# Attention cut into single-block steps, with the steps behind it carried on between the expert units

## The chip, the cores and the metric

The kernel is one program on one core of one Trainium2 chip. The metric is the device time of one execution in microseconds (us), median of three. The engines are named as in the profile: PE (TensorE, matrix products and transposes), PEld (its weight loads), DVE (VectorE), ACT (ScalarE), POOL (GpSimd), SP (SyncE, which issues DMAs here). Each engine runs its own instructions strictly in their order and waits for the others through semaphores.

## The reference, cut to what matters

Sixteen batches of 512 rows of 128 numbers, all fp32, go through two residual branches.

```python
h = layernorm(x) * (1 + ca) + sa
x = x + ga * attention(h)      # rows routed to 2 of 8 experts; q, k, v; chunked linear attention per expert,
                               # at most 256 rows of an expert; two parts weighted and summed; norm per head; o_w
h = layernorm(x) * (1 + cb) + sb
x = x + gb * ffn(h)

# ffn(h):
h = h @ lin0_w + lin0_b
h = silu(h @ swi1_w1 + b1) * (h @ swi1_w2 + b2)
scores = softmax(h @ gate_w.T);  topv, topi = top_k(scores, 4);  combine = topv / sum(topv), scattered over 8
g = silu(einsum('td,edh->eth', h, exp_w1)) * einsum('td,edh->eth', h, exp_w3)
routed = einsum('te,etd->td', combine, einsum('eth,ehd->etd', g, exp_w2))
h = routed + silu(h @ sh_w1) * (h @ sh_w3) @ sh_w2      # shared part, 2 x 128 hidden
h = h @ lin1_w + lin1_b
h = silu(h @ swi2_w1 + b1) * (h @ swi2_w2 + b2)
```

## The kernel before

A batch is four tiles of 128 rows. The program is a row of blocks of code (`nc.Block()`); all engines leave one before any enters the next.

1. **Preparation** (lines 241 to 636). Loads, layer norm, q products and logits in 17 steps of one batch each (`steps`, from `step` on each engine), then two rounds of routing on DVE (`route`), which give each row its place. POOL scatters the rows of the first four batches to DRAM, sorted by expert.
2. **Attention** (lines 741 to 1292). The sorted rows make 160 blocks of 128 rows. A loop runs over *pairs* of blocks (`for g in ITERATIONS`). PE turns the rows (`turn`, L966), forms k and v (`keys_values`, L978), turns k (`turn_k`, L985), forms the scores (`scores`, L995, both blocks of a pair at once, into the four banks of `wide`), the state k'v (`states`, L1016), adds the carried state (`carried`, L1027) and the scores times v (`attend`, L1035), and turns the result (L1046). ACT copies from PSUM. DVE masks scores (`mask_scores`, L1142) and q (L1162), multiplies k (L1136) and sums states (L1154); POOL masks the summed state by heads (`sum_masked`, L756), which PE's `carried` needs.
   Once the blocks of a batch are stored, the batch has *later steps*: POOL gathers its rows (L765) and adds halves (L778), ACT weights them, DVE normalises, PE turns, multiplies by `o_w`, `lin0`, the two `swi1` matrices and the router's matrix (L1051, L1058, L1102), DVE adds the residual (L1223) and finishes the hidden rows (L1237). A table `J1` gives each batch a slot; slot = block number, a batch starts its PE steps every `PERIOD` = 10 slots, the first at slot 58, the last at 208, and `at(step, slot)` says which batch has that step there. The blocks end at slot 159, so the loop goes on to slot 226 with later steps alone.
3. **Router** (lines 1316 to 1382). The choice of four experts for the rest of the rows on DVE, exponent and turned weights, the split of all expert weights into a high and a low part (ACT L1335, POOL L1328), the weights to DRAM.
4. **Experts** (lines 1426 to 1570). 160 units, ten a batch (eight experts, two shared halves): PE forms gate and up (`up`, L1471, three matmuls each), ACT applies Silu (L1532), POOL multiplies by the row weights that a DMA has spread over the partitions (L1437), DVE multiplies gate and up (`ep`, L1568), ACT and DVE split the product into high and low (L1537, L1561), PE adds the unit's share three units later (`down`, L1481). The last products of the batch before (`tail`, L1488 to L1498) stand in units 3, 4, 5 and 7.

## Time and profile before

| | us |
|---|---|
| runs of before | 1444.19, 1449.04, 1450.40; median 1449.04 |
| profiled execution, its own time | 1450.58 |
| span of its instructions | 1448.8 |
| PE busy | 1127.1 (78%) |
| DVE busy | 875.1 (60%) |
| ACT busy | 683.7 (47%) |
| POOL busy | 586.2 (40%) |

The span is the time from the first to the last instruction of the profiled execution; 1.8 us of its own time lie around it. Busy shares are averages over four stages of different kinds. The time of a stage is read from the start of its first instruction to that of the next stage, and inside a stage from the distance between two starts of the same line. Mean granted clock of PE: 0.88 of full speed (full is 2.4 GHz, the other level 1.2 GHz).

### The profile page before, as it was taken

What the parts mean: (1) busy time and instruction counts of PE and PEld (TensorE: products, weight loads), DVE (VectorE), ACT (ScalarE), POOL (GpSimd) and SP (SyncE); (2) the same over time, 40 slices, a digit from 0 to 9 for tenths busy, and PEclk for the clock granted to TensorE, in tenths of its full rate; (3) what the DMA queues carried; (4) which work ended last, traced back from release to release, by engine and by line L of the source; (5) the groups of instructions that cost most, each with busy time, mean ns of one, the idle gap of its engine ahead of it and who ended that gap; (6) DMA issues with size and microseconds to landing.
All of it is one profiled execution on the core that took longest, in us unless ns stands there. A gap on an engine that the chain in (4) does not pass through costs nothing. (4 is left out here: it accounts for less than half of the span.)

```text
span 1448.8 us, 27085 instructions
## 1 busy us (share of the span) xinstructions
PE 1127.1 (78%) x9330; PEld 802.7 (55%) x9330; DVE 875.1 (60%) x1823; ACT 683.7 (47%) x1653; POOL 586.2 (40%) x626
## 2 busy tenths in 40 slices
PE   2891118889877888888898885663699999999997
PEld 2671006666655565555666652321477777777774
DVE  5447275666456666665777767325366666666664
ACT  1460004555445565555666653332355555555553
POOL 1003403442555445554333335503245454545541
PEclk8895559999898999999999995555699999999997
DMA  9921112332332222222222111100432332424220
GB/s 310 390 113 47 69 48 77 103 90 78 97 89 83 72 79 87 84 84 66 71 58 67 56 35 29 27 3 0 123 107 83 96 101 78 118 66 131 66 73 14
DMA packets 83536, 125.71 MB, mean 87 GB/s; under 512 B 9041, under 2 KB 65873, under 8 KB 79313
## 3 DMA queue, kind: packets, MB, share of 16 engines
q1 hardware_dynamic: 73168, 98.86, 22.6%
q0 software_dynamic: 10240, 25.18, 5.4%
q8 instruction: 76, 1.25, 0.4%
q14 instruction: 52, 0.42, 0.1%
HBM read 71.32 MB, written 52.69 MB: 86 GB/s over the span
## 5 line engine op out<-in xcount | busy, mean ns | idle before, releaser
L1142 DVE SCALAR_TENSOR_TENSOR att<-reach,endrel,wide 128x1024 f32<-128x1024 f32 x160 | 204.4, 1277 | 197.0 <-PE wide L995 146.1
L1437 POOL TENSOR_TENSOR eg<-eg,hq 128x512 f32<-128x512 f32 x128 | 172.7, 1355 | 211.6 <-ACT eg L1532 183.4
L1561 DVE TENSOR_TENSOR epp<-ep,epp 128x512 fp32r<-128x512 f32 x160 | 148.9, 930 | 131.4 <-ACT epp L1537 129.9
L199 POOL DMA_INDIRECT routed_rows<-hq,idxs x128 | 132.5, 1035 | 189.3 <-DVEq L611 117.3
L756 POOL TENSOR_TENSOR sm<-su,headm 128x128 f32<-128x128 f32 x160 | 76.2, 476 | 289.4 <-DVE su L1154 287.7
L978 PE MATMUL bank<-kvw,turned 128*128 x320 | 148.9, 547 | 32.8 <-DVE kf L1136 25.3
L1481 PE MATMUL bank<-epp,w2p 128*128 128x512 f32 x480 | 156.4, 434 | 2.9 <-DVE epp L1561 2.9
L1537 ACT ACTIVATE epp<-ep 128x512 fp32r<-128x512 f32 x160 | 100.8, 630 | 104.9 <-DVE ep L1568 104.9
L765 POOL DMA_INDIRECT gst<-attended_rows,idxs x128 | 133.5, 1043 | 33.5 <-issue 32.8
L850 ACT ACTIVATE k1s<-bank 128x128 f32<-128x128 f32 x160 | 44.4, 278 | 181.7 <-PE bank L978 173.4
L995 PE MATMUL wide<-turned,kx 32*128 32x128 f32 x2560 | 108.9, 291 | 5.9 <-ACT kx L864 3.6
L1481 PEld LDWEIGHTS bank<-epp,w2p 128*128 128x128 f32 x480 | 89.5, 189 | 40.1 <-issue 21.3
L995 PEld LDWEIGHTS wide<-turned,kx 32*128 32x128 f32 x2560 | 90.2, 189 | 26.0 <-ACT kx L864 16.7
L1471 PE MATMUL bank<-hp,w1p 128*128 128x512 f32 x321 | 93.3, 400 | 9.5 <-DVE ep L1568 5.6
L864 ACT ACTIVATE kx<-bank,parity 128x256 f32<-128x256 f32 x160 | 66.9, 469 | 64.5 <-PE bank L985 62.2
L1035 PE MATMUL bank<-att,vx 128*32 128x128 f32 x2560 | 91.3, 286 | 0.0
L1471 PE MATMUL wide<-hp,w3p 128*128 128x512 f32 x318 | 90.0, 391 | 0.0
L978 PEld LDWEIGHTS bank<-kvw,turned 128*128 128x128 f32 x320 | 48.7, 191 | 59.9 <-issue 52.3
L1532 ACT ACTIVATE eg<-bank 128x512 f32<-128x512 f32 x107 | 62.8, 587 | 31.0 <-PE wide L1471 15.9
L1035 PEld LDWEIGHTS bank<-att,vx 128*32 128x32 f32 x2560 | 68.4, 114 | 12.5 <-issue 6.1
L1471 PEld LDWEIGHTS bank<-hp,w1p 128*128 128x128 f32 x321 | 61.6, 193 | 23.8 <-DVE ep L1568 6.0
L1568 DVE TENSOR_TENSOR ep<-wide,eg 128x512 f32<-128x512 f32 x106 | 72.1, 681 | 0.0
(269 smaller groups left out, 2166.2 us busy)
## 6 DMA issues: line engine op xcount, KB each, us to landing
hq<-weight_rows SPq DMA_DIRECT2D x16, 2048.0 KB, 9.7
routed_rows<-zero SPq DMA_DIRECT2D x4, 5120.0 KB, 24.5
rows<-routed_rows SPq DMA_DIRECT2D x80, 256.0 KB
attended_rows<-ob SPq DMA_DIRECT2D x80, 128.0 KB
out<-fin SPq DMA_DIRECT2D x16, 256.0 KB, 2.5
routed_rows<-hq,idxs POOLq DMA_INDIRECT x128
gst<-attended_rows,idxs POOLq DMA_INDIRECT x128
kw_raw<-in_k_w SPq DMA_DIRECT2D x1, 512.0 KB, 5.3
```

What stands on the lines that cost most here:

```text
L199: pool.indirect_dma_start(hs[s], bass.IndirectOffsetOnAxis(idxs[:, t, k:k + 1], 0), hq[:, t, :], None, bounds_check=BLOCKS[s] * P - 1, oob ...
L756: pool.tensor_tensor(sm[:, n % 4, :], su[:, n % 4, :], headm[:, :], ALU.mult).then_inc(s_sm, 1)
L765: pool.indirect_dma_start(gst[:, u, k, :], None, orow[s], bass.IndirectOffsetOnAxis(idxs[:, b * NT + k // TOPA, k % TOPA:k % TOPA + 1], 0) ...
L978: pe.matmul(bank[1][:, 0:KV], turned[:, n // 2 % 2, 0, n % 2, :], kvw[:, bass.ds(w, KV)], start=True, stop=True).then_inc(s_kv, 1)
L995: mm = pe.matmul(wide[:, p, (2 * a + par) * P:(2 * a + par + 1) * P], kx[r, par, a * P:(a + 1) * P], turned[r, g % 2, 1, a, :], start=True ...
L1035: mm = pe.matmul(bank[2][32 * p:32 * p + 32, n % 2 * P:(n % 2 + 1) * P], vx[:, n % 4, p, par * DK:(par + 2) * DK], att[:, n % 2, p, par * ...
L1142: dve.scalar_tensor_tensor(out=att[:, n % 2, :, :], in0=reach[:, :, :].rearrange("p a c -> p (a c)").unsqueeze(1) .to_broadcast([P, 4, 2 * ...
L1437: pool.tensor_tensor(g, g, rows_of(b % 2, n, n + 1), ALU.mult).then_inc(s_eu, 1)
L1471: mm = pe.matmul(ps[:, :], w[:, wk, n, :], hp[:, b % 2, hk, :], start=(wk + hk == 0), stop=(hk == 1))
L1481: mm = pe.matmul(bank[0][:, :], w2p[:, wk, n, :], epp[:, k % RING, hk, :], start=(n + wk + hk == 0), stop=(n == NU - 1 and hk == 1))
L1537: act.activation(epp[:, (k - 1) % RING, 0, :], ep[:, (k - 1) % RING, :], ACT.Copy).then_inc(s_eh, 1)
L1561: dve.tensor_tensor(epp[:, (k - 1) % RING, 1, :], ep[:, (k - 1) % RING, :], epp[:, (k - 1) % RING, 0, :], ALU.subtract).then_inc(s_el, 1)
```

## The change

- **Attention by blocks.** The loop runs over single blocks (`ITERATIONS = range(-6, NBK)`). Scores are formed and masked one block at a time, in one half of the four banks, one block ahead of `attend`; k and v are formed five blocks ahead of it (three at most before). `rows` and `turned` have three buffers, `kx` two, `vx` six. The head mask goes from the summed state (POOL) to the state before the sum, for two blocks at once, on DVE (`mask_states`). `kf`, `km`, `qm`, `sm` lie in tiles of `hq`, so DVE waits for the first scatters before it clears buffers. The table begins later: first PE steps at slot 86, then every 10 slots.
- **Later steps run on among expert units.** The loop ends at slot 159. `post_pool`, `post_act`, `post_pe`, `post_freed` and `post_dve` are shared functions, and expert unit k calls them with slot 160 + k. The last batch has its router product at slot 252, unit 92. On DVE the steps are cut smaller and spread over more slots, and the adding of halves moves from POOL to DVE.
- **Router by four.** Once four batches have their logits, 33 small DVE operations over the next slots choose and weight them, ACT takes the exponent in between (it needs another table and Silu's again afterwards: four pairs of table loads, three of them among the expert units), PE turns four batches at once. Block 3 is gone.
- **Weights split early.** `w1s`, `w3s`, `w2s` are loaded into the last tiles of `hq`, and ACT (before step 8 of preparation) and POOL split them there; ACT waits for POOL before step 12.
- **Experts.** Gate products have two banks instead of three, since bank 3 belongs to the later steps, so `up(k)` also waits for the Silu of unit k - 2. A step's product or transposes end the unit on PE. POOL makes the hidden rows' parts of batches 0 and 1 at the start of this block.

```diff
+                for n, (w, parts) in enumerate(((w1s, w1p), (w3s, w3p), (w2s, w2p))):
+                    pool.wait_ge(s_wh, n + 1)
+                    pool.tensor_tensor(parts[:, 1, :, :], w[:, :, :], parts[:, 0, :, :],
+                                       ALU.subtract).then_inc(s_wl, 1)
...
-                steps(act, step)
+                def split_weights():
+                    act.wait_ge(s_w1, 16 * NW1)
+                    for w, parts in ((w1s, w1p), (w3s, w3p), (w2s, w2p)):
+                        act.activation(parts[:, 0, :, :], w[:, :, :], ACT.Copy).then_inc(s_wh, 1)
+
+                steps(act, step, split_weights, lambda: act.wait_ge(s_wl, 3))
...
-        PERIOD, GATHER = 10, 16
+        PERIOD, GATHER, CHAIN, ROUTE = 10, 19, 10, 33
+        J1 = [C0[1] + 46 + PERIOD * b for b in range(NB)]
...
-                    pool.tensor_tensor(sm[:, n % 4, :], su[:, n % 4, :], headm[:, :], ALU.mult).then_inc(s_sm, 1)
...
+                def mask_states(g):
+                    dve.wait_ge(s_st, g + 1)
+                    if g:
+                        dve.wait_ge(s_sm, 2 * g)
+                    dve.tensor_tensor(sh[:, :, :], bank[3][:, 0:2 * P].rearrange("p (a c) -> p a c", c=P),
+                                      headm[:, :].unsqueeze(1).to_broadcast([P, 2, P]), ALU.mult).then_inc(s_sh, 1)
...
+                for n in ITERATIONS:
+                    h, odd = divmod(n, 2)
+                    if is_block(n + 1):
+                        scores(n + 1)
+                    if is_block(n):
+                        attend(n)
+                    if not odd and here(h + 1):
+                        states(h + 1, n)
+                    if is_block(n + 5):
+                        keys_values(n + 5)
+                    if not odd and here(h + 3):
+                        turn(h + 3)
+                    if odd and here(h):
+                        turn_outputs(h)
+                    if odd and here(h + 2):
+                        turn_k(h + 2)
+                    if not odd and here(h + 1):
+                        pe.wait_ge(s_sh, h + 2)
+                    post_pe(pe, n)
+                    if is_block(n + 1):
+                        carried(n + 1)
...
-        gate_bank = (bank[1], bank[2], bank[5])
-        up_bank = (bank[3], bank[4], bank[6])
+        gate_bank = (bank[1], bank[2])
+        up_bank = (bank[4], bank[5], bank[6])
...
+                    if k >= 2:
+                        pe.wait_ge(s_es, k - 1)
...
                     if BEHIND <= k < UNITS + BEHIND:
                         down(k - BEHIND)
+                    post_pe(pe, NBK + k)
```

PE in the attention, one pair of blocks without later steps, in the order before (`wide` holds the scores, `kvw` the k and v matrices, `ident` marks a transpose):

```order
L995 MATMUL wide<-turned,kx 128x128 x16
L978 ISA
L978 MATMUL bank<-kvw,turned 128x384
L966 MATMUL bank<-ident,rows 128x128 x4
L1016 MATMUL bank<-vx,km 128x128 x2
L1046 MATMUL bank<-ident,oTs 128x128 x2
L978 ISA
L978 MATMUL bank<-kvw,turned 128x384
L1027 MATMUL bank<-qm,sm 128x128 x2
L985 MATMUL bank<-ident,kf 128x128 x2
L1035 MATMUL bank<-att,vx 32x128 x16
```

And the same pair in the changed kernel, two passes of the loop (`hq` now holds kf, km, qm and sm):

```order
L1235 MATMUL wide<-turned,kx 128x128 x8
L1270 MATMUL bank<-att,vx 32x128 x8
L1253 MATMUL bank<-vx,hq 128x128 x2
L1210 ISA
L1210 MATMUL bank<-kvw,turned 128x384
L1199 MATMUL bank<-ident,rows 128x128 x4
L1262 MATMUL bank<-hq 128x128
L1235 MATMUL wide<-turned,kx 128x128 x8
L1270 MATMUL bank<-att,vx 32x128 x8
L1210 ISA
L1210 MATMUL bank<-kvw,turned 128x384
L1224 MATMUL bank<-ident,oTs 128x128 x2
```

The sixteen score products became two groups of eight, each followed at once by the `attend` of the block before, and `turn_k` (L1217, right behind the last row shown) no longer stands two rows behind the k product that it needs.

PE in the experts, two units of before with nothing of a batch's tail:

```order
L1471 MATMUL bank<-hp,w1p 128x512 x3
L1471 MATMUL bank<-hp,w3p 128x512 x3
L1481 MATMUL bank<-epp,w2p 128x512 x3
L1471 MATMUL bank<-hp,w1p 128x512 x3
L1471 MATMUL wide<-hp,w3p 128x512 x3
```

And four units of the changed kernel (L797 turns, L804 multiplies; both are later steps of another batch):

```order
L1466 MATMUL bank<-epp,w2p 128x512 x3
L797 MATMUL bank<-ident,gst 128x128 x4
L1456 MATMUL bank<-hp,w1p 128x512 x3
L1456 MATMUL wide<-hp,w3p 128x512 x3
L1483 MATMUL wide<-ident,t 128x128 x4
L1466 MATMUL bank<-epp,w2p 128x512 x3
L804 MATMUL bank<-jt,oT 128x512
L1456 MATMUL bank<-hp,w1p 128x512 x3
L1456 MATMUL wide<-hp,w3p 128x512 x3
L1466 MATMUL bank<-epp,w2p 128x512 x3
L797 MATMUL bank<-ident,jm 128x128 x4
```

Eight of ten units end with a piece of a later step.

DVE in the experts, two units of before:

```order
L1561 TENSOR_TENSOR epp<-ep,epp 128x512
L1568 TENSOR_TENSOR ep<-bank,eg 128x512
L1546 SCALAR_TENSOR_TENSOR t<-wide,bias,tg 128x512
L1561 TENSOR_TENSOR epp<-ep,epp 128x512
L1568 TENSOR_TENSOR ep<-wide,eg 128x512
```

And two of the changed kernel, in a batch that also has router pieces (`choice`, `top`; `kvw` now holds eg and ep):

```order
L1549 TENSOR_TENSOR epp<-kvw,epp 128x512
L1556 TENSOR_TENSOR kvw<-wide,kvw 128x512
L958 TENSOR_REDUCE var<-gst 128x32
L962 TENSOR_SCALAR var<-var 128x32
L968 BN_STATS bst<-x_all 128x6 x4
L928 TENSOR_TENSOR choice<-choice,top 128x128
L932 TENSOR_TENSOR choice<-choice 128x128
L934 SCALAR_TENSOR_TENSOR choice<-choice 128x128
L1549 TENSOR_TENSOR epp<-kvw,epp 128x512
L1556 TENSOR_TENSOR kvw<-wide,kvw 128x512
```

The later steps stand between the product of one unit and the split of the next operand.

## Rows read from the trace of the kernel before

**Rows 1.** Windows by stage: us, busy by engine with counts, clock, DMA share, GB/s.

```profile
108.00:209.00 101.00, 13.22 (x132) 9.62 (x132) 61.17 (x150) 2.59 (x5) 32.03 (x32) 0.52 0.12 42
355.00:865.00 510.00, 429.63 (x5307) 307.50 (x5311) 331.66 (x751) 288.35 (x842) 237.55 (x291) 0.97 0.25 74
865.00:993.00 128.00, 84.56 (x209) 37.86 (x198) 52.95 (x181) 45.48 (x101) 39.41 (x37) 0.53 0.07 18
993.00:1026.00 33.00, 3.77 (x17) 2.32 (x17) 23.61 (x34) 7.85 (x9) 12.61 (x7) 0.50 0.03 8
1061.00:1410.00 349.00, 334.90 (x1408) 258.06 (x1407) 233.85 (x310) 189.20 (x337) 183.61 (x141) 1.00 0.31 90
```

**Rows 2.** Timeline, first state sum of block 0 and of block 40: start, duration.

```profile
224.58 0.35 DVE L1154 SCALAR_TENSOR_TENSOR su<-su,carry,bank 128x128 f32<-128x128 f32 x1 [0.88 <-PE bank L1016]
359.84 0.35 DVE L1154 SCALAR_TENSOR_TENSOR su<-su,carry,bank 128x128 f32<-128x128 f32 x1
```

**Rows 3.** Timeline, residual added for batches 0, 9, 11 and 15.

```profile
448.49 0.68 DVE L1223 TENSOR_TENSOR x_all<-bank,x_all 128x512 f32<-128x512 f32 x1
831.20 0.68 DVE L1223 TENSOR_TENSOR x_all<-bank,x_all 128x512 f32<-128x512 f32 x1
889.63 0.69 DVE L1223 TENSOR_TENSOR x_all<-bank,x_all 128x512 f32<-128x512 f32 x1
968.84 0.69 DVE L1223 TENSOR_TENSOR x_all<-bank,x_all 128x512 f32<-128x512 f32 x1 [8.18 <-PE bank L1051]
```

**Rows 4.** Timeline, one pair of blocks without later steps.

```profile
337.31 1.17 PE L995 MATMUL wide<-turned,kx 32*128 32x128 f32 x32
338.55 1.28 DVE L1142 SCALAR_TENSOR_TENSOR att<-reach,endrel,wide 128x1024 f32<-128x1024 f32 x1 [2.04 <-PE wide L995]
340.25 0.79 DVE L1154 SCALAR_TENSOR_TENSOR su<-su,carry,bank 128x128 f32<-128x128 f32 x2
341.11 0.52 PEld L1027 LDWEIGHTS bank<-qm,sm 128*128 128x128 f32 x4 [0.43 <-DVE su L1154]
342.14 0.28 DVE L1136 TENSOR_TENSOR kf<-bank,k1s 128x128 f32<-128x128 f32 x1
342.34 0.60 DVE L1162 SCALAR_TENSOR_TENSOR qm<-column,erel,turned 128x128 f32<-128x128 f32 x2
342.48 0.14 PEld L985 LDWEIGHTS bank<-ident,kf 128*128 128x128 f32 x1 [0.79 <-DVE kf L1136]
343.75 1.17 PE L995 MATMUL wide<-turned,kx 32*128 32x128 f32 x32
```

**Rows 5.** Timeline, starts of expert units around a product, four transposes, and neither.

```profile
1164.45 0.85 PE L1471 MATMUL bank<-hp,w1p 128*128 128x512 f32 x3
1167.39 0.85 PE L1471 MATMUL bank<-hp,w1p 128*128 128x512 f32 x3
1172.40 0.84 PE L1471 MATMUL bank<-hp,w1p 128*128 128x512 f32 x3
1174.89 0.86 PE L1471 MATMUL bank<-hp,w1p 128*128 128x512 f32 x3
1176.95 0.84 PE L1471 MATMUL wide<-hp,w1p 128*128 128x512 f32 x3
```

**Rows 6.** Page, costliest groups: busy us, mean ns, idle before and its releaser.

```profile
L1437 POOL TENSOR_TENSOR eg<-eg,hq 128x512 f32<-128x512 f32 x128 | 172.7, 1355 | 211.6 <-ACT eg L1532 183.4
L1561 DVE TENSOR_TENSOR epp<-ep,epp 128x512 fp32r<-128x512 f32 x160 | 148.9, 930 | 131.4 <-ACT epp L1537 129.9
```

**Rows 7.** Timeline of the router block: weights split, a DVE operation beside it.

```profile
994.88 1.25 ACT L1335 ACTIVATE w3p<-w3s 128x1280 fp32r<-128x1280 f32 x1
995.05 2.89 POOL L1328 TENSOR_TENSOR w1p<-w1s,w1p 128x1280 fp32r<-128x1280 f32 x1 [43.55 <-ACT w1p L1335]
995.28 2.88 DVE L228 TENSOR_TENSOR fw<-fw,fa 128x192 f32<-128x192 f32 x1
997.31 1.28 ACT L1337 ACT_TABLE_LOAD   x1
```

More of the change, by code:

```diff
@@ new lines, in adaln_block @@
+        gst = kept("gst", [P, 2, NT * TOPA, D])
+        NV = NT * H + NT
+        var = kept("var", [P, NV])
+        inv = kept("inv", [P, NV])
+        tmp = kept("tmp", [P, NV])
+        offset = kept("offset", [P, NT])
+        jt = kept("jt", [P, S])
+        jh = kept("jh", [P, S])
+        jm = kept("jm", [P, S])
+        js = kept("js", [P, S])
+        bst = kept("bst", [P, NT, 6])
+        mv = kept("mv", [P, NT, 2])
+        RT = 4 * NT
+        left, one, equal, picked, ex = (kept(f"choice{i}", [P, RT, E]) for i in range(5))
@@ L739, in at, with group, halves_of, post_pool @@
             return b if rest == 0 and 0 <= b < batches else None
-        def here(g):
-            return 0 <= g < PAIRS
-        ITERATIONS = range(-2, LAST // 2 + 1)
-        with nc.Block() as block:
-            @block.gpsimd
-            def _(pool):
-                def sum_masked(n):
-                    pool.wait_ge(s_su, n + 1)
-                    if n >= 3:
-                        pool.wait_ge(s_o, (n - 3) // 2 + 1)
-                    pool.tensor_tensor(sm[:, n % 4, :], su[:, n % 4, :], headm[:, :], ALU.mult).then_inc(s_sm, 1)
-                def gather(b, k):
+        def group(step, slot):
+            b = at(step + 16, slot)
+            return b // 4 if b is not None and b % 4 == 3 else None
+        def halves_of(b):
+            return gst[:, b % 2, :, :].rearrange("p (i s) d -> p i s d", s=TOPA)
+        def post_pool(pool, slot):
+            for k in range(NT * TOPA):
+                b = at(k - GATHER, slot)
+                if b is not None:
                     u, s = b % 2, sum(b >= x for x in B0[1:])
@@ new lines, in adaln_block, with here, is_block, _ @@
+        s_a = sem("scores_masked")
+        s_st = sem("states_ready")
+        s_sh = sem("states_masked")
+        s_sm = sem("states_summed")
+        s_o = sem("attended")
+        s_oc = sem("attended_copied")
+        s_ot = sem("attended_turned")
+        s_oe = sem("attended_rows_ready")
+        def here(g):
+            return 0 <= g < PAIRS
+        def is_block(n):
+            return 0 <= n < NBK
+        ITERATIONS = range(-6, NBK)
+        with nc.Block() as block:
+            @block.gpsimd
+            def _(pool):
+                sent = [NT * TOPA * B0[1]]
+                def scatters(n):
@@ new lines, in turn_k, with turn_outputs, scores @@
+                    mm.then_inc(s_kt, 1)
+                def turn_outputs(g):
+                    pe.wait_ge(s_oc, g + 1)
+                    pe.wait_ge(s_te, min(g + 4, PAIRS))
+                    for a in range(2):
+                        mm = pe.transpose(bank[0][:, (2 + a) * P:(3 + a) * P], oTs[:, a * P:(a + 1) * P], ident[:, :])
+                    mm.then_inc(s_ot, 1)
+                def scores(n):
+                    pe.wait_ge(s_kx, n // 2 + 1)
+                    if n:
+                        pe.wait_ge(s_a, n)
+                    a = n % 2
+                    for par in range(2):
+                        for p in range(4):
+                            r = slice(32 * p, 32 * p + 32)
+                            mm = pe.matmul(wide[:, p, par * P:(par + 1) * P], kx[r, n // 2 % 2, par, a * P:(a + 1) * P],
+                                           turned[r, n // 2 % 3, 1, a, :], start=True, stop=True)
@@ L1018, in states @@
+                    for slot in (n - 2, n - 1):
+                        if group(12, slot) is not None:
+                            pe.wait_ge(s_wc, group(12, slot) + 1)
+                    for m in (2 * g, 2 * g + 1):
+                        pe.wait_ge(s_km, m + 1)
+                        pe.wait_ge(s_ve, m + 1)
+                        mm = pe.matmul(bank[3][:, m % 2 * P:(m % 2 + 1) * P], km[:, m % 4, :], vx[:, m % 6, :, 0:DK],
                                        start=True, stop=True)
@@ new lines, in attend @@
+                def attend(n):
+                    pe.wait_ge(s_a, n + 1)
+                    v = vx[:, n % 6, :, :].rearrange("q h c -> q (h c)")
+                    for par in range(2):
+                        for p in range(4):
+                            mm = pe.matmul(bank[2][32 * p:32 * p + 32, n % 2 * P:(n % 2 + 1) * P],
+                                           v[:, (4 * p + par) * DK:(4 * p + par + 2) * DK],
+                                           att[:, n % 2, p, par * P:(par + 1) * P], start=False, stop=True,
+                                           skip_group_check=True)
+                    mm.then_inc(s_o, 1)
@@ L1429, in _ @@
             def _(pool):
+                for b in range(2):
+                    hidden_parts(pool, b, b)
                 for k in range(UNITS):
@@ L1556, in _ @@
                     b, n = divmod(k, NU)
+                    post_freed(dve, NBK + k)
                     if b:
```

994 lines of the change are left out of this document (445 added, 549 removed).

## Prediction

> **What bounds the kernel now.** I read the windows by stage first [rows 1]. From 355 to 865 us (attention with later steps) PE is busy 84% of the time at a granted clock of 0.97, DVE 65%; in the experts (1061 to 1410) PE is busy 96% at 1.00, DVE 67%. Between them lie 161 us in which nothing is full: 865 to 993, the later steps of the last six batches or so, PE busy 66% at clock 0.53, and 993 to 1026, the router, PE 11%. From 108 to 209 DVE's routing sets the pace (61.17 us busy) and POOL's scatters.
>
> Then the distances of repeated lines. Blocks without later steps: 40 blocks in 359.84 - 224.58 = 135.3 us, 33.8 per ten [rows 2]. With them: nine batches, ninety blocks, in 831.20 - 448.49 = 382.7, 42.5 per ten; later steps alone: (968.84 - 889.63) / 4 = 19.8 per batch [rows 3]. Later steps therefore cost 8.7 us a batch beside blocks and 19.8 alone. In a pair without them (6.44 us from scores to scores) PE's loads wait 0.43 for the state sum, since POOL masks it, and 0.79 for kf; DVE waits 2.04 for the scores [rows 4]. So the pair is a loop of waits, not a full engine.
>
> **The change, part by part.** All of it is against the profiled execution: span 1448.8, own time 1450.6, which is 1.5 above the median of the runs shown; I treat them as equal.
>
> *Work of a pair, first.* PE: 6.44 less the two waits is 5.2 us. DVE: two masks of 1.28, 0.79, two of 0.28 and 0.60 make 4.5 [rows 4]; the new head mask (two blocks, 256 columns, one operand in PSUM) lies between kf's 0.28 (128 columns) and the residual's 0.68 (512) [rows 3, 4], I take 0.42, so 4.9. *Later steps on PE:* a unit with a product lasts 1167.39 - 1164.45 = 2.94, one with four transposes 1174.89 - 1172.40 = 2.49, a plain one 1176.95 - 1174.89 = 2.06 [rows 5]: 0.88 a product, 0.43 a turn. Four products, three turns and the router's eight short matmuls (estimate 0.8) make 5.6 a batch at full clock. *Later steps on DVE:* 52.95 busy in the tail for 6.5 batches, 8.1 a batch with the choices [rows 1]; plus the adding of halves (0.7, as the residual's 0.68), plus about 2 because the choices come in pieces of four batches: 9 to 11.
>
> *Preparation.* ACT's three copies cost 1.25 each, 3.8 us in a loop whose steps follow closely. POOL's three subtractions last 2.9 each, and beside the first a small DVE operation lasted 2.88, as long as POOL's own [rows 7]. In the changed kernel the normalising operations of DVE stand beside them. So between +4 (copies alone) and +12 (copies and all of POOL's 8.7): I take +6.
> The Trainium skill (SBUF — State Buffer, Who interferes with whom) says that a DVE operation with two SBUF inputs is blocked for the whole of a GpSimd instruction that reads SBUF. The row with 2.88 agrees. It speaks against putting these subtractions there.
>
> *Filling the loop.* First state sum 15.6 us after the block began (209 to 224.58) [rows 1, 2]. The new loop has two more single passes before block 0 and clears buffers only after the scatters: 0 to +5, I take +3.
>
> *Attention.* All the waits just named get a block or more of distance: scores are masked while PE does `attend` of the block before, the sum needs no POOL, kf is made a pass ahead. What remains is the larger engine. Later steps reach DVE at slot 77. Until then, 77 blocks at the larger of 2.6 (PE) and 2.45 (DVE) plus some coupling: I take 2.8, 216 us. From there 83 blocks: PE 26 + 5.6 = 31.6, DVE 24.7 + 9 to 11 = 34 to 36 per ten, so DVE becomes the bound there, at 3.5 a block, 291 us. Together 507 against 865 - 224.58 = 640: **-133**. The bounds: PE's work alone is 160 x 2.6 + 7 x 5.6 = 455 (-185); at the old pace with fewer later steps in it, 77 x 3.38 + 83 x 4.25 = 613 (-27).
>
> *The tail and the router.* 128 + 33 = **-161** [rows 1]. The weights' split and the first hidden rows that lay in the router block are the terms above and below.
>
> *Experts.* Slots 160 and later hold 72 of the 128 PE steps (batch 6 has three left, batch 7 five, eight batches all): nine batches' worth. PE is full here, so each costs at least 5.6 (+51). A batch there is 100 matmul records (90, three products of two, four turns), and 1408 of them in 349 us make 24.8 us a batch; DVE's 233.85 make 16.6 of it [rows 1]. Plus 9 to 11 is 26 to 28, plus what POOL's multiplications block (L1561 lasts 0.93 in the mean, the residual's operation of the same size with an input in PSUM 0.68 [rows 3, 6]) about 30, next to PE's 30.4. Two nearly full engines with waits between them: I take 7 a batch, **+63**. Upper bound: the pace of later steps alone, 9 x 19.8 = +178. POOL now makes two hidden parts at the start, under the loads of the weight rows. Three pairs of table loads of 1.28 [rows 7] hold ACT 2.6 us each; units have a slack of three, so +2 each with the other small things, **+7** with what the start costs. The new wait on Silu of unit k - 2 comes a whole unit after that product; I give it nothing, and if ACT falls a unit behind it costs PE what ACT is late.
>
> Sum: 1448.8 + 6 + 3 - 133 - 161 + 63 + 7 = 1233.8; with 1.8 around the span 1235.6. Waits that I can't see are likelier than gains, so I say **1240**.
>
> **Rivals.**
> *A. The blocks gain little.* `wide` is now used one half at a time: scores of block n + 2 wait until DVE has masked n + 1, and on DVE head mask, q mask, kf, sum and the later steps stand in between. For it: DVE's load of later steps is cut in more and smaller pieces, and each waits for its own end. Against it: DVE's row shows it idle 2.04 a pair now. If the pace stays that of before, the attention is 613: 1240 + 106 = 1346, and half of it 1293.
> *B. DVE sets the pace in the experts.* POOL computes 8 x 1.36 for the experts of a batch [rows 6] and two more operations of that size for the hidden parts, 13.6 us. If DVE is blocked for all of that instead of the 2.5 that L1561 shows now (ten at 0.93 instead of 0.68), a batch lasts 16.6 + 10.3 + 11.1 = 38: nine of them cost 13.2 each instead of 7, 1240 + 56 = 1296.
> The Trainium skill's rule above would make this of it, since additions, inversions and router choices mostly have two SBUF inputs, reductions not.
> *C. The clock falls in the experts.* The tail ran at 0.53 with PE busy 66% of the time, the experts at 1.00 with 96%, the attention at 0.97 with 84% [rows 1]. If the later steps' waits open gaps in PE's queue, a batch's 30.4 us of PE work becomes 61. Nine batches cost 275: 1515, slower than before; it decides from 209 / 30.4, seven batches at the lower level. Against it: the attention of before has such gaps and kept 0.97.
> The Trainium skill (TensorE: Matmul & The Clock Gate, HAM oscillation) says that idle gaps of PE between bursts bring the lower clock back each time. That is this rival's rule.
> *D. The steps don't hide.* ACT and DVE take later steps in their queues, so a late gather or a late transposed tile holds the unit behind it. Each batch would cost its stand-alone 19.8: 1240 + 115 = 1355.
> *E. Better than I think.* PE alone bounds both stages: attention at -185, experts at +51: 1240 - 52 - 12 = 1176.
>
> **How the numbers follow.** The forecast, 1200 to 1285, has 0.62; A at or near its full price 0.13; B or D from 1285 up 0.12; E below 1200 0.09; C or something else as bad 0.03; the change not doing what it says (the tail's and router's 161 us coming back as a stall at the start of the experts) 0.01. The likeliest's own range is 1200 to 1285; with half of A and most of B taken in, the range is 1195 to 1315. About 0.5% is what a measurement of this kernel can tell. Faster has 0.96: all but C and the last, since even A, or D, ends 90 us below 1450. Same 0.01, slower 0.03.
>
> **What would show it.** No stretch of the trace with PE below half busy between the first block and the first expert unit, except the wait for the weight rows. Distances of state sums of about 28 us per ten blocks early and 35 late; DVE above 90% busy in the late half. Ten units with later steps in 31 to 33 us, without them 24.8 again, clock 1.00. The steps of preparation 5 to 8 us longer around the split, with normalising operations of nearly 3 us. My forecast is wrong if a pair still takes above 6.4 us early (A), if expert batches take 36 or more (B, D), or if the clock's row in the experts shows stretches at half (C).

## The result: slower, 1494.7 us against 1448.7

The changed kernel took 1494.68 us (median of 4, 1490.13 to 1499.51), the kernel before beside it 1448.72: ratio 1.032, 95% interval 1.028 to 1.037. The forecast was 1240, with 0.03 for slower. The profiled run has a span of 1497.8 us and a mean granted clock of 0.865.

The windows by stage answer to [rows 1]. Columns: window, its length, then busy time and instructions of each engine, granted clock, DMA share, GB/s. The stretches are the routing, the start of the attention, its first 40 blocks, a stretch between two of them, nine batches of the experts with later steps, five without.

```profile
108.00:215.00 107.00, 18.90 (x176) 14.43 (x173) 63.74 (x157) 6.57 (x11) 31.94 (x32) 0.54 0.11 40
215.50:284.20 68.70, 14.34 (x48) 8.35 (x48) 3.61 (x9) 6.72 (x18) 51.85 (x54) 0.50 0.36 123
284.20:424.40 140.20, 123.42 (x1664) 90.64 (x1668) 90.61 (x181) 70.41 (x218) 10.35 (x11) 0.91 0.23 66
424.40:490.40 66.00, 35.51 (x428) 24.68 (x424) 22.68 (x46) 17.56 (x55) 29.45 (x29) 0.74 0.24 72
979.80:1300.20 320.40, 281.76 (x1135) 202.69 (x1136) 255.88 (x490) 190.71 (x361) 166.92 (x140) 0.94 0.29 79
1332.70:1457.80 125.10, 120.76 (x500) 91.05 (x499) 85.73 (x118) 67.34 (x121) 65.65 (x50) 1.00 0.28 80
```

In the page's costliest groups (busy time and mean ns of one, then idle time before them and what ended most of it), the masks of the scores and the gathers read:

```profile
L1312 DVE SCALAR_TENSOR_TENSOR att<-reach,endrel,wide 128x1024 f32<-128x1024 f32 x160 | 204.8, 1280 | 177.1 <-remote 120.6
L735 POOL DMA_INDIRECT gst<-attended_rows,idxs x128 | 134.0, 1047 | 549.7 <-PE bank L797 387.9
```

The tail and the router's block (161 us) are gone, and the preparation is 6.7 us longer, both near the forecast. But the first scores are masked at 284.2, 69 us after the attention began at 215.4, and between blocks 40 and 50 (424 to 490) PE is busy 35.5 of 66 us. Undisturbed blocks go at 30.0 us per ten; the holes ahead of block 0 (about 50 us), between 40 and 50 (36) and between 80 and 90 (20) have no counterpart before. The first ten blocks, with 50.0 us, and the blocks from 90 to 100, with 52.1, are stretched too. In the hole ahead of block 0 the timeline of VectorE, and then ScalarE's, of the changed kernel reads (start, length, engine, line; in brackets the idle time before, and what ended it):

```profile
233.13 0.34 DVE L1330 SCALAR_TENSOR_TENSOR hq<-hq,carry,sh 128x128 f32<-128x128 f32 x1
284.25 1.28 DVE L1312 SCALAR_TENSOR_TENSOR att<-reach,endrel,wide 128x1024 f32<-128x1024 f32 x1 [50.77 <-remote]
```
```profile
241.34 0.39 ACT L1150 ACTIVATE hq<-hq,kmask 128x128 f32<-128x128 f32 x1
289.84 0.28 ACT L1131 ACTIVATE k1s<-bank 128x128 f32<-128x128 f32 x1 [48.11 <-remote]
```

VectorE waits for scores whose last product, by the records, ended at 233.7; ScalarE for a key product that ended at 243.2. The trace also records when each semaphore is raised. The one for the scores is raised at 284.22, 50.5 us behind the end of the product, and VectorE goes 0.03 us later; the one for the keys at 289.82, 46.6 us behind. In the same trace the median of the 160 score signals is 0.04 us behind the product. So the instruction that should raise the semaphore has run by its record, and the semaphore is raised 50 us late. (The ends of products are modelled, and the trace doesn't tell whether the result itself is written late or only the word of it.) "remote" is, as I read it, the profile's word where no instruction of this core ended at the right moment to be the releaser. What runs meanwhile is GpSimd:

```profile
236.63 0.97 POOL L204 DMA_INDIRECT routed_rows<-hq,idxs  x1 [0.30 <-issue]
237.91 0.97 POOL L204 DMA_INDIRECT routed_rows<-hq,idxs  x1 [0.31 <-issue]
...
429.46 1.04 POOL L735 DMA_INDIRECT gst<-attended_rows,idxs  x1 [131.86 <-DMA attended_rows<-ob]
430.80 1.01 POOL L735 DMA_INDIRECT gst<-attended_rows,idxs  x1 [0.30 <-issue]
...
438.62 1.00 POOL L735 DMA_INDIRECT gst<-attended_rows,idxs  x1 [0.30 <-issue]
439.92 1.04 POOL L204 DMA_INDIRECT routed_rows<-hq,idxs  x1 [0.30 <-issue]
```

Before, `sum_masked` on GpSimd waited for every block's state sum, and the scatters and gathers stood between those waits. The change moved the masking to VectorE, and nothing ties GpSimd to the blocks any more. It issues 64 scatters in a row, one per 1.28 us, until about 297; then it stands 131.9 us at the first gather, which wants the first slots' rows stored, and does all that has piled up in a second row from 429 on. The holes lie where the rows lie: the third beside two rows of 18 and 17 from 607 and from 661 on.

### The profile page after: what moved, and what is told of

It is laid out like the page before. It is cut to its first block and busy times, and to the rows that moved or that the text cites. A ratio compares the mean times of both kernels' runs of the same rounds, so it can differ in the third digit from the quotient of the medians.

```text
span 1497.8 us, 27081 instructions
## 1 busy us (share of the span) xinstructions
PE 1141.7 (76%) x9330; PEld 811.5 (54%) x9330; DVE 926.2 (62%) x1990; ACT 687.2 (46%) x1662; POOL 481.6 (32%) x450
## 3 DMA queue, kind: packets, MB, share of 16 engines
q8 instruction: 78, 1.28, 0.4%
## 5 line engine op out<-in xcount | busy, mean ns | idle before, releaser
L1421 POOL TENSOR_TENSOR kvw<-kvw,hq 128x512 f32<-128x512 f32 x128 | 170.5, 1334 | 227.5 <-ACT kvw L1518 221.6
L1549 DVE TENSOR_TENSOR epp<-kvw,epp 128x512 fp32r<-128x512 f32 x160 | 149.6, 935 | 96.2 <-ACT epp L1523 94.2
L1456 PE MATMUL bank<-hp,w1p 128*128 128x512 f32 x480 | 161.0, 444 | 4.6 <-POOL hp L1372 4.6
L1523 ACT ACTIVATE epp<-kvw 128x512 fp32r<-128x512 f32 x160 | 100.5, 628 | 94.3 <-DVE kvw L1556 85.8
L1456 PE MATMUL wide<-hp,w3p 128*128 128x512 f32 x480 | 140.9, 402 | 0.0
L1518 ACT ACTIVATE kvw<-bank 128x512 f32<-128x512 f32 x160 | 94.4, 590 | 80.9 <-PE wide L1456 78.9
L1556 DVE TENSOR_TENSOR kvw<-wide,kvw 128x512 f32<-128x512 f32 x160 | 109.1, 682 | 20.7 <-POOL kvw L1421 20.7
L1456 PEld LDWEIGHTS wide<-hp,w3p 128*128 128x128 f32 x480 | 92.6, 193 | 22.9
L1305 DVE TENSOR_TENSOR hq<-bank,k1s 128x128 f32<-128x128 f32 x160 | 46.5, 291 | 91.4 <-ACT vx L1134 63.1
L1262 PE MATMUL bank<-hq 128*128 128x128 f32 x320 | 66.7, 292 | 24.2 <-DVE sh L1322 24.2
```

What stands on the lines that cost most here:

```text
L1421: pool.tensor_tensor(g, g, rows_of(b % 2, n, n + 1), ALU.mult).then_inc(s_eu, 1)
L1456: mm = pe.matmul(ps[:, :], w[:, wk, n, :], hp[:, b % 2, hk, :], start=(wk + hk == 0), stop=(hk == 1))
L1523: act.activation(epp[:, (k - 1) % RING, 0, :], ep[:, (k - 1) % RING, :], ACT.Copy).then_inc(s_eh, 1)
L1549: dve.tensor_tensor(epp[:, (k - 1) % RING, 1, :], ep[:, (k - 1) % RING, :], epp[:, (k - 1) % RING, 0, :], ALU.subtract).then_inc(s_el, 1)
L1556: dve.tensor_tensor(ep[:, k % RING, :], up_bank[k % RING][:, :], eg[:, k % RING, :], ALU.mult).then_inc(s_ep, 1)
```

## The experiments

One thing has to be known first. The kernel before took 1442 to 1450 us in the median beside some sets of these runs and 1360 to 1363 beside others, and the sets ran on different chips (three of the one sort, two of the other, besides the first measurement, which is of the first sort). I call them slow-signal and quick-signal chips, for what is shown below; runs are compared within a sort alone. No chip was seen to be of both sorts, and the one that was used twice was quick both times; but that it is the chip, and not something else that goes on beside the kernel there, was not tested.

### Pacing GpSimd again

```
 for n in ITERATIONS:
+    if is_block(n + 4):                 # e4: and n < 83
+        pool.wait_ge(s_kf, n + 5)
     post_pool(pool, n)
     scatters(n)
```


> The changed kernel, with one wait more: GpSimd waits in each attention iteration for the key features of four blocks ahead, so that its scatters and gathers are spread over the blocks again, as before the change. Theory S (an unbroken row of GpSimd's indirect DMAs keeps the other engines from getting their next instructions): the three holes between blocks (50 us ahead of block 0, 36 between blocks 40 and 50, 20 between 80 and 90, 106 in all) go, and a part of each later ten blocks, where eight gathers stand in a row: 1494.7 - 106 = 1389 us, and some 5 us less for each of eight batches, 1350. Rival O (the new order of the steps, three row buffers in place of four): nothing changes, 1480 to 1500. Rival P (GpSimd's work blocks VectorE's port): the same number of indirect DMAs costs the same, 1480 or more.

> As the paced kernel, but only in iterations below 83, in which the scatters are; the gathers behind them still stand in a row of eight. Theory S: the three holes go, the blocks from 96 on still take 47.8 us per ten: about 1380 us, 15 to 30 us above the paced kernel. If the rows of eight gathers do no harm: the same time as the paced kernel within 5 us. Rivals O and P: 1480 to 1500.

Both came to a quick-signal chip: 1284.46 us (ratio to before 0.946, 0.943 to 0.950) and 1281.20 (0.942, 0.940 to 0.945), beside 1360.35 of the kernel before. That does not decide, because the changed kernel itself was not there. So it was run, unchanged, with the paced one:

> The changed kernel itself, unchanged. The kernel before took 1360 us beside the last runs where it had taken 1449, and the bare scatters left no hole there, so a part of what was to be tested may hang on the chip or its state. Theory S without such a dependence: 1494.7 us and the three holes, so about 1400 where the kernel before takes 1360. Theory S with it (the scatters keep the other engines from their instructions on the one chip and not on the other): where the kernel before takes 1360, no holes and about the time of the paced kernel, 1275 to 1300; where it takes 1449, 1495 again.

> The paced kernel once more, on the same chip as the changed kernel unchanged. Where the kernel before takes 1360 us: 1284 again, and within 10 us of the changed kernel if that has no holes there. Where it takes 1449: theory S says 1350 to 1390, 100 us or more below the changed kernel; rivals O and P say the changed kernel's own time.

These two met a slow-signal chip: changed kernel 1497.83 (ratio 1.033, 1.029 to 1.037), paced 1358.43 (0.936, 0.933 to 0.938). One added wait makes the kernel **139 us faster** there. The waits of the unchanged one (line waited for, by whom, total, times, longest) hold the same holes again:

```profile
DVE att L1312 <- remote: 135.3, 11, 49.5
ACT k1s L1131 <- remote: 103.2, 8, 46.8
```

In the paced kernel the first is 3.1 us in one time, and the second isn't there. By the trace's semaphore records, 12 of the 160 score signals of the unchanged kernel come more than 2 us behind their product, and one of the paced kernel's (3.1 us). Rival O (the order, the three row buffers) and rival P (VectorE's port) fall for the holes: the order and the number of DMAs are the same. The changed kernel on a quick-signal chip came later:

> The changed kernel, unchanged, for the comparison within this set. Where the kernel before takes 1449 us: 1495. Where it takes 1360: theory S with its dependence on the chip says 1275 to 1300, no holes; without it 1400.

1286.18 us, one run, beside 1362.29: 0.944, and 1284 to 1286 paced. GpSimd issues the same 64 scatters in a row there, from 186 to 266 us, and none of the 160 score signals comes more than 0.1 us behind its product. On those chips there is nothing to pace; the same change is a gain of 5.6% there and a loss of 3.2% here. What the rows of eight gathers cost was to be read from e4, which did not meet a slow-signal chip; beside them ten blocks from block 110 on take 46 to 49 us unpaced and 39 to 42 paced.

### Does a row in the kernel before do the same?

```
-    pool.tensor_tensor(sm[:, n % 4, :], su[:, n % 4, :], headm[:, :], ALU.mult)
+    dve.tensor_tensor(sm[:, n % 4, :], su[:, n % 4, :], headm[:, :], ALU.mult)
```


> The kernel before, with the masking of the summed states moved from GpSimd to VectorE (128 products of about 0.35 us), so that GpSimd waits for no block any more and issues its scatters in a row. Theory S: a hole of 40 us or more ahead of or in the first blocks, and one or two more at the next slots, 1448.7 + 60 to 110 = 1510 to 1560 us. Rival O: only VectorE's 45 us of work, partly hidden: 1450 to 1475.

1384.84 on a quick-signal chip, one run, 24 us over the kernel before and without a hole (the products moved to VectorE are 160, 39.2 us in all, not 128). It says only that such chips don't mind; on a slow-signal chip it wasn't tried. But the kernel before has the effect in small there: 50.7 us of "remote" waits of VectorE in 15 times, and the hole of the preparation, below.

### What is it that comes late?

First theory: the other engines' next instructions. Bare operations beside bare scatters (e3 and e7; e11 has 768 operations of 8 columns and 48 turns):

```
 for part in range(2):                  # GpSimd, behind each phase
     for i in range(48): scatter(...)
 for i in range(592): op(...)           # VectorE, ScalarE; a drain after 8
 for 37 turns: 16 x op(...)             # the third phase, a loop
```


> The preparation of the changed kernel, and behind it no attention and no experts, but three phases in which VectorE and ScalarE do 592 independent products (copies) of 128 columns each: written out without any scatter, written out beside 48 scatters in a row on GpSimd, and as a loop of 37 turns of 16 beside 48 scatters in a row. Theory S, by way of the instructions that each engine has to be sent: no hole in the first phase, one of 20 to 60 us on each engine in the second (as long as the scatters last), none in the third. Rival P (port): the second and the third are slowed alike, operation by operation, and ScalarE is not. Rival O: no holes in any.

> The bare scatters once more (preparation, then three phases of 592 independent operations on VectorE and ScalarE: written out without scatters, written out beside 48 scatters in a row, as a loop beside 48 in a row). Where the kernel before takes 1360 us: no hole, as in its first run. Where it takes 1449: if what the engines lack in a hole is their next instructions, no hole in the first phase, one of 20 us or more on VectorE and on ScalarE in the second, none in the loop; if it is the access to SBUF or PSUM (rival P), the second and the third phase are slowed alike; if it is something of the attention alone, none is.

> The bare scatters with shorter operations: 768 independent operations of 8 columns a phase on VectorE and on ScalarE (about 0.1 us each), so that a row of 48 scatters (61 us) lies beside some 500 instructions of each engine instead of 200. Phase one written out without scatters, phase two written out beside them, phase three as a loop of 48 turns of 16 beside 48 more. Where the kernel before takes 1360 us: no hole. Where it takes 1449: if the engines lack instructions, holes in phase two alone, which end with the scatters (20 to 50 us on both engines), phase three within 10% of phase one; if they lack access to memory, phases two and three both longer by the same share.

The first two met quick-signal chips: no drain above 1.75 us in any phase. The third met a slow-signal chip. Its waits in a stretch of the row of phase two, and then in phase three (the loop):

```profile
DVE dve_scratch L695 <- issue: 51.5, 9, 10.5
ACT act_scratch L699 <- issue: 48.0, 9, 10.3
POOL routed_rows L204 <- issue: 15.0, 48, 0.6
```
```profile
ACT act_scratch L699 <- issue: 55.4, 9, 10.8
DVE dve_scratch L695 <- issue: 50.2, 9, 10.1
```

And VectorE's timeline there: eight operations, 0.7 us, and then ten of nothing.

```profile
333.91 0.89 DVE L695 TENSOR_TENSOR dve_scratch<-column,headm 128x8 f32<-128x8 f32 x8 [8.45 <-issue]
345.11 0.71 DVE L695 TENSOR_TENSOR dve_scratch<-column,headm 128x8 f32<-128x8 f32 x8 [10.31 <-issue]
355.61 0.71 DVE L695 TENSOR_TENSOR dve_scratch<-column,headm 128x8 f32<-128x8 f32 x8 [9.80 <-issue]
```

Each ten is the `drain` behind eight operations: the instruction that the program puts there to wait until the engine's operations before it are done. It lasts up to 11.4 us while scatters come in a row, from about 5 us behind the row's beginning (VectorE's are 1.2, 4.0, 2.6, 6.0, 8.8, 10.5, 10.2, 10.9 us), and under 1.0 in phase one. These are the durations of the drains' own records, so a drain has begun and doesn't end; with missing instructions it would begin late. It lasts as long in the loop, where I had expected no hole, and in the attention the semaphore itself is raised late. So the theory of missing instructions falls for the drains and for the holes. What comes late is the confirmation that an engine's work is done. That late drains and late semaphores are one effect is my inference: both come beside rows of scatters on slow-signal chips alone. TensorE is held up too, without a semaphore in between, and for that row, which is no loop, late instructions are not excluded: in the preparation, beside the row of 32, counting products that follow each other within 0.1 us otherwise come 0.7 to 2.1 us apart (paced kernel, slow-signal chip):

```profile
169.52 0.19 PE L459 MATMUL bank<-selb,ones 128*128 128x40 bf16 x1 [1.22 <-issue]
171.63 0.19 PE L459 MATMUL bank<-selb,ones 128*128 128x32 bf16 x1 [1.92 <-issue]
173.72 0.18 PE L459 MATMUL bank<-selb,ones 128*128 128x24 bf16 x1 [1.90 <-issue]
```

### How long a gap is enough?

```
     scatter(pool, ...)                 # in the attention (e8, e14); in the bare loop (e15)
+    pool.memset(gap_work[:, :], 0.0)
+    pool.drain()
```


> The changed kernel, without the paced kernel's wait; GpSimd clears a scratch tile of 384 columns (about 0.4 us) and drains behind each scatter in the attention, so that 64 scatters take some 110 us in place of 82. It tells whether gaps are enough or whole pauses are wanted. Where the kernel before takes 1449 us: if any gap lets the instructions through, the three holes go and 1385 to 1400 us remain (the rows of eight gathers stay as they are); if the other engines wait until the row of transfers is over, the first hole grows to about 75 us: 1520 to 1560. Where it takes 1360: within 5 us of the changed kernel there.

> The changed kernel with about 0.4 us of other work of GpSimd behind each scatter of the attention, again, for a chip with holes (the kernel before at 1449 us): 1385 to 1400 if any gap lets the instructions through, 1520 to 1560 if the engines wait for the end of the longer row. Where the kernel before takes 1360: about 1322 again, which the first holes of that kernel must explain otherwise.

> The bare short operations again, but in the third phase (the loop) GpSimd clears 384 columns and drains behind each of the 48 scatters, so that one comes every 1.8 us or so in place of 1.28. Where the kernel before takes 1440 us or more: second phase (scatters in a row) drains of up to 10 us, as before. Third phase: if any gap lets the ends of writes through, no drain of VectorE or ScalarE above 2 us; if it is the bytes in flight that count, drains of 3 to 8 us. Where the kernel before takes 1360: no drain above 2 us in any phase.

On a slow-signal chip the changed kernel with gaps took 1394.43 (one run, before 1441.8): the first two holes are gone. The third only moved: the blocks from 70 to 100 take 138.9 us, against 135.4 unpaced and 123.9 paced, with nine gathers of GpSimd in a row there at 457 us. The rows of eight gathers still cost what they did (from block 110 on ten blocks beside them take 46 to 48 us, 39 to 42 in the paced kernel). The gap is larger than I expected: the memset is 0.44, the drain's record is 2.7 long and overlaps that of the next DMA, and scatters come 3.26 us apart, with 2.3 us from the end of one to the start of the next. In the bare kernel with the same gaps, the phase with the row (above) and the phase with gaps (below):

```profile
DVE dve_scratch L699 <- issue: 55.0, 8, 10.5
ACT act_scratch L703 <- issue: 51.7, 8, 10.3
```
```profile
DVE dve_scratch L699 <- issue: 19.9, 47, 0.5
ACT act_scratch L703 <- issue: 12.6, 47, 0.3
```

No hole at all, with the same 48 scatters; the longest drain is 0.7 us. On a quick-signal chip the gaps only cost: 1322.08, 36 us more than without them where I had expected 5, and as I read it because GpSimd's queue is full and the gathers behind the scatters come late (ScalarE waits 33.7 us for gathered rows between 440 and 620).

> The paced kernel, and in the preparation a pause too: GpSimd waits behind its 8th scatter until TensorE's second group of counting products is done (147 us in the paced kernel on the chip without holes; on the other it ended at 179, beside 32 scatters in a row). Theory S, where the kernel before takes 1449 us: the 30 us of that hole go, if the other 24 scatters meet no engine that needs instructions: 1358 - 30 = 1328 us, at least 1345. Rival (the late counting has a cause of its own on that chip): 1358. Where the kernel before takes 1360: within 5 us of 1284.

> The paced kernel, and the same work of GpSimd (0.4 us and a drain) behind each of the 32 scatters of the preparation. Where the kernel before takes 1440 us or more: the counting products end at about 148 us in place of 179, and the routing behind them at about 187 in place of 215, when the scatters too are done: 1358 - 25 = 1333 us, between 1325 and 1345. If the hole in the preparation has another cause: 1358. Where the kernel before takes 1360: 1284 to 1292, since the last of the scatters comes just when VectorE is done.

> The paced kernel, with a gap of about 2 us (a small memset and a drain of GpSimd) behind every fourth scatter of the preparation. Where the kernel before takes 1440 us or more: the row of 32 ends 16 us later, at about 187, the counting products end at 148 to 155 in place of 177, the routing at 185 to 195 in place of 212: 1358 - 20 = 1338 us, between 1328 and 1350. If rows of four are already too long: 1358 to 1375. Where the kernel before takes 1360: 1284 to 1292.

> The changed kernel without the paced kernel's waits, with the same gap behind every fourth scatter in the preparation and in the attention, and in every fourth iteration in which the gathers are. Where the kernel before takes 1440 us or more: if the length of a row alone decides, the three holes of the attention and the one of the preparation go, 1340 to 1365 us; if waits for the blocks are wanted, 1380 to 1450. Where it takes 1360: 1284 to 1295.

e9 (a wait in the preparation) met a quick-signal chip: 1286.31, ratio 0.945. e16 met a slow-signal one, with gaps in the preparation as well. I had expected 1325 to 1345, and it is slower than paced alone: 1389.17 (0.958, 0.954 to 0.962). The counting products are whole again,

```profile
146.53 0.82 PE L465 MATMUL bank<-selb,ones 128*128 128x128 bf16 x16
176.03 0.78 PE L469 MATMUL bank<-ends,sel 128*128 128x120 f32 x2 [28.68 <-DVEq L618]
```

and VectorE's routing ends at 184 in place of 212. So the hole of the preparation, which the kernel before has too (its counting products end at 172.7 us), comes from the row of scatters as well. But the 32 scatters now last until about 236, and the attention waits for them. e17 and e18 (gaps behind every fourth) were meant to mend that; both met a quick-signal chip, 1289.57 (0.947) and 1291.51. What they do on the other sort wasn't seen.

### Why a batch of the experts takes 35.6 us

```
-    act.activation(ex[:, :, :], ex[:, :, :], ACT.Exp)
+    act.activation(ex[:, :, :], ex[:, :, :], ACT.Copy)            # e12
-    pool.tensor_tensor(g, g, rows_of(b % 2, n, n + 1), ALU.mult).then_inc(s_eu, 1)
+    pool.sem_inc(s_eu, 1)                                          # e13
```


> The paced kernel with the later steps' router exponent as a plain copy, so that ScalarE needs no other table (the routed weights are then others). If the table loads hold the experts' units up: the batches in which a group of four is routed (the 2nd, and the 5th and 6th: 40, 37 and 41 us beside 33 to 34 of the others) lose 2 to 3 us each, 6 to 8 us together. If it is the chain of small operations on VectorE that does it: less than 2 us together.

> The paced kernel without GpSimd's products of the experts' gates by the routed weights (eight a batch; left out, so that VectorE's product follows ScalarE's Silu directly; the sum over experts is then unweighted). If these products block VectorE beside them, and hold up the chain from Silu to the product: a batch with later steps falls from 35.6 to 32 us or less, nine batches 30 us or more. If TensorE is what lacks (it is busy 31.7 of the 35.6): a batch stays above 34.5. Batches without later steps stay at 24.9 in either case.

Both ran once, on a slow-signal chip; against the paced kernel's 1358.43, e12 took 1357.08 and e13 1322.15. Windows of the same nine batches, the paced kernel first, then without the exponent, then without GpSimd's products:

```profile
842.30:1161.00 318.70, 283.59 (x1135) 203.81 (x1136) 259.27 (x489) 190.90 (x361) 166.96 (x140) 0.93 0.28 79
```
```profile
840.50:1157.20 316.70, 282.99 (x1135) 203.27 (x1136) 258.28 (x489) 185.25 (x357) 170.10 (x140) 0.95 0.29 80
```
```profile
841.10:1132.10 291.00, 274.10 (x1135) 198.64 (x1136) 206.58 (x489) 187.75 (x361) 73.45 (x68) 0.97 0.32 89
```

Table loads are worth 2 us over nine batches; the second and sixth batch still took 40 us. Leaving GpSimd's products out is worth 27.7, 3.1 a batch, where I had expected 30 or more, and VectorE is busy 52.7 us less with the same 489 instructions. It takes more away than what they do to VectorE: a unit no longer waits for GpSimd between Silu and product, and the granted clock is 0.97 in place of 0.93. (Without later steps, at clock 1.00 in both, a batch goes from 24.9 to 24.0.) Three of VectorE's lines, with the products (above) and without:

```profile
L1551 DVE TENSOR_TENSOR epp<-kvw,epp 128x512 fp32r<-128x512 f32 x90 | 87.1, 968 | 44.7 <-ACT epp L1525 43.6
L900 DVE SCALAR_TENSOR_TENSOR inv<-tmp,inv 128x36 f32<-128x36 f32 (+1 forms) x27 | 18.0, 668 | 0.6
L895 DVE TENSOR_TENSOR tmp<-inv 128x36 f32<-128x36 f32 (+1 forms) x27 | 11.0, 407 | 0.6
```
```profile
L1550 DVE TENSOR_TENSOR epp<-kvw,epp 128x512 fp32r<-128x512 f32 x90 | 62.2, 691 | 58.6 <-ACT epp L1524 58.0
L895 DVE TENSOR_TENSOR tmp<-inv 128x36 f32<-128x36 f32 (+1 forms) x27 | 8.0, 297 | 0.6
L900 DVE SCALAR_TENSOR_TENSOR inv<-tmp,inv 128x36 f32<-128x36 f32 (+1 forms) x27 | 6.0, 222 | 0.6
```

One operation of 36 columns (L900) lasts three times as long beside GpSimd's 1.3 us products. The Trainium skill (SBUF — State Buffer, Who interferes with whom) says that a VectorE operation with two inputs in SBUF contends with a GpSimd instruction that reads SBUF; these rows agree with it, and the product with an input in PSUM did not change (682 and 684 ns). Not every line fits so well: L897, also with two inputs in SBUF, lasts 245 ns with the products and 290 without.

The windows of single batches say more. In the paced kernel, the fourth and the fifth batch, which hold the same kinds of steps, and then the second:

```profile
949.50:982.80 33.30, 30.21 (x129) 21.66 (x128) 28.27 (x50) 21.60 (x42) 21.63 (x19) 1.00 0.37 100
982.80:1019.10 36.30, 32.15 (x130) 23.38 (x129) 28.74 (x51) 21.55 (x42) 20.98 (x19) 0.91 0.30 81
872.90:913.50 40.60, 33.81 (x134) 23.75 (x132) 35.02 (x78) 25.06 (x46) 23.63 (x20) 0.92 0.26 73
```

With the same work on VectorE and ScalarE, a batch at a granted clock of 0.91 takes 3.0 us more than one at 1.00; five of the nine batches are at 0.92 or below. In the second batch VectorE is the fullest engine, 35.0 of 40.6 us. Without the exponent that batch ran at a clock of 1.00 and still took 40.3; without GpSimd's products it took 36.8, with VectorE busy 29.1. That points to VectorE's load with the router's small operations, and not to the clock or the tables; no run took those operations out.

## Why the prediction was wrong

The miss is 255 us, and the runs split it. Unpaced to paced on slow-signal chips: 139. (In that set the changed kernel took 3 us more than in the first.) From the paced 1358 to the forecast 118, of which the attention has 82 (589.0 from the first mask to the last against 507), the experts 33 (318.7 less nine times 31.8), and 3 the rest.

**Right:** the tail and the router, -161; batches without later steps at 24.9 to 25.0 us. The preparation's number is right too, +6 against 6.7, but its sign is missing: none of VectorE's operations between 60 and 124 us lasts a microsecond, though GpSimd's three subtractions of 2.9 us lie there, so the number is in part luck. Rival C did not come as priced, no batch fell to half clock; in small it did, with 0.93 in the mean of the batches with later steps and about 3 us on those at 0.91.

**The step that failed first:** "the sum needs no POOL", priced as a wait that goes. That wait was also what spaced GpSimd's indirect DMAs, and without it a row of them kept the other engines' signals back by up to 50 us: 139 us in all. I asked what VectorE's new work costs, and not what GpSimd does once nobody holds it: none of my terms has its scatters in it, though their rows were in the trace. Where I named what would show me wrong (a pair above 6.4 us, batches of 36 or more, the clock), the stretch with PE below half busy stood in my list for the right reading only. That a row of DMAs delays other engines could not be read from any row that I showed, but 50.7 us of "remote" waits stood in the waits of before, and I passed over them.

**The attention's size, a gain too large:** "6.44 less the two waits is 5.2 us". Two idle times of the weight loads, which overlap with products, were taken off the pair as if the pair were one chain; in that very pair (337.31 to 343.75) PE was busy 5.89 us. The windows answer directly. The kernel before over 40 blocks, and the changed kernel over 60 on a quick-signal chip:

```profile
224.58:359.84 135.26, 121.90 (x1680) 88.55 (x1679) 86.68 (x160) 72.34 (x219) 52.22 (x72) 1.00 0.30 90
```
```profile
203.20:383.00 179.80, 178.19 (x2506) 131.96 (x2510) 135.99 (x270) 105.81 (x328) 78.41 (x80) 1.00 0.39 120
551.80:710.20 158.40, 148.96 (x1800) 104.62 (x1804) 125.86 (x321) 102.00 (x297) 34.02 (x32) 1.00 0.23 65
```

PE was busy 3.05 us a block before and is busy 2.97 now, not 2.6: the blocks gained what was idle (3.38 to 3.00) and stand at PE's floor, 99% busy. With later steps it is 94% busy, at 39.6 us per ten, where I had 35 with VectorE as the bound; VectorE is at 79%. On the quick-signal chip, whose signals are not late, the attention is 539.5 us, 32 above my 507. The other 50 of the 82 are the difference between the sorts of chip that stays with pacing (589.0 against 539.5): the paced kernel still issues up to four DMAs in a row (155 of the 256 alone), and its waits hold 25.7 us of ScalarE's for outputs and 11.2 of VectorE's under "remote". That these are the whole 50 was not shown.

**The experts, rival B in part:** nine batches at 35.4 to 35.6. GpSimd's products block VectorE for 5.9 us a batch (52.7 / 9), where my forecast held 2.5 of it and B the whole 13.6. Leaving them out gives back 3.1 of the 3.6 us that were missing, the rise of the clock included; how it divides between the blocked VectorE, the shorter way from Silu to product and the clock was not told apart. The batches with the router's small operations take 40, with VectorE as the fullest engine; it isn't the table loads.

So rival A was half right (the blocks gain little, but for PE's own work and not for the single half of `wide`), B half, and the rival that won, slower through a freed GpSimd, was not among them.

The best kernel seen on both sorts is the changed one with one wait for GpSimd: 0.936 of the kernel before on the one, 0.946 on the other.

## What to carry to other kernels

A wait that is taken away may have been pacing what stands behind it in its queue: list that queue, and ask what it looks like issued in one row, above all if it is GpSimd's indirect DMAs, the only ones tried here. A floor is busy time per unit of work from the windows, not a unit's length less its waits. And a gain on one chip can be a loss on the next: time the kernel before again beside every set.

## What the hardware showed that I had not expected

- On some chips a row of GpSimd's scatters (128 rows of 1 KB each, one per 1.28 us) goes with drains of VectorE and ScalarE of up to 11.4 us in place of under 1.0, with TensorE's products 0.7 to 2.1 us apart, and with semaphores raised as much as 50 us late; on others none of it, with the same kernel (score signals within 0.1 us). With 2.3 us between scatters (3.26 from one to the next) no drain is late, and with rows of four at most in the attention no score signal is more than 3.1 us late. What it is that is occupied below that, and why chips differ, is open.
- The DMA engines are far from full meanwhile: a busy share of 0.36 at 123 GB/s in the first hole.
- Beside GpSimd products of 1.3 us, one of VectorE's 36-column operations (L900, two inputs in SBUF) lasted 668 ns in the mean instead of 222.
- Batches of experts with the same work took 33.3 us at a granted clock of 1.00 and 36.3 at 0.91.
